# Row maxima of two attention heads, taken together from two neighbouring PSUM banks

## The reference

```python
q = _heads(xq @ wq)
k, v = jnp.split(ctx @ wkv, 2, axis=-1)
...
sim = jnp.einsum('bhnd,bhmd->bhnm', q, k) * DH ** (-0.5)
a = jax.nn.softmax(sim, axis=-1)
o = jnp.einsum('bhnm,bhmd->bhnd', a, v)
```

## Time and profile before

| | us |
|---|---|
| median of three runs | 6196.47 |
| lowest, highest | 6185.82, 6211.56 |
| profiled execution | 6242.82 |
| its span | 6241.0 |

### The profile page before, as it was taken

The page is one execution under the profiler, slowest core; times in us unless marked ns, Lnnn a source line. Parts: engine busy times, 40 slices in busy tenths (PEclk is TensorE's granted clock), DMA queues, the critical chain, the costliest instruction groups (busy, mean ns, idle before and its releaser), DMA issues. The chain is left out here.

```text
span 6241.0 us, 170025 instructions
## 1 busy us (share of the span) xinstructions
PE 5692.5 (91%) x66584; PEld 3349.0 (54%) x66584; DVE 4360.4 (70%) x8986; ACT 3383.1 (54%) x7674; POOL 2505.9 (40%) x2223
## 2 busy tenths in 40 slices
PE   6999899988899989998889998999888998899988
PEld 4566346643556635664356653566435665356633
DVE  6886666656788666665788867666668886666664
ACT  3455565546544556554644556555564555655555
POOL 2566016730256501673026640277103663037700
PEclk9999699987899969998899987999779998699976
DMA  4000010000100001000010000100001000010000
GB/s 111 23 16 17 13 30 16 13 20 12 44 23 16 15 15 32 14 14 18 16 44 22 16 18 12 32 13 15 19 17 45 13 16 17 11 36 13 7 17 8
DMA packets 277771, 135.56 MB, mean 22 GB/s; under 512 B 151005, under 2 KB 266301, under 8 KB 276862
## 3 DMA queue, kind: packets, MB, share of 16 engines
q1 hardware_dynamic: 276990, 124.68, 8.5%
HBM read 101.90 MB, written 3.01 MB: 17 GB/s over the span
## 5 line engine op out<-in xcount | busy, mean ns | idle before, releaser
L2266 DVE TENSOR_REDUCE max_part<-ring 128x1 f32<-128x400 f32 (+2 forms) x4608 | 2418.6, 578 | 776.1 <-PE ring L1425 768.0
L1918 ACT ACTIVATE probs<-ring 128x512 f32<-128x512 f32 (+1 forms) x4096 | 2101.2, 572 | 1337.9 <-PE ring L1425 1312.4
L1401 POOL TENSOR_TENSOR weight_sum<-weight_sum,probs 128x512 f32<-128x512 f32 (+1 forms) x1408 | 1793.7, 1274 | 150.3 <-ACT probs L1918 11.5
L1425 PE MATMUL o_acc<-probs,region 128*32 128x256 f32 (+2 forms) x13312 | 1503.1, 441 | 47.2 <-ACT probs L1918 41.4
L1425 PEld LDWEIGHTS o_acc<-probs,region 128*32 128x32 f32 (+2 forms) x13312 | 617.2, 133 | 573.8 <-issue 262.4
L1401 POOL TENSOR_TENSOR weight_sum<-probs 128x512 f32<-128x512 f32 x256 | 332.1, 1297 | 1467.7 <-PE ring L1425 923.6
L1425 PE MATMUL ring<-qop,region 64*128 64x256 f16 x9984 | 833.1, 270 | 22.6 <-ACT shift_q L1763 16.7
L1763 ACT ACTIVATE region<-ring 65x128 f32<-65x128 f32 (+4 forms) x1232 | 560.9, 474 | 413.8 <-PE ring L1425 319.8
L1425 PE MATMUL ring<-nk,nq 32*128 32x400 f16 (+2 forms) x2560 | 601.9, 401 | 65.2 <-ACT probs L1918 51.1
L1425 PEld LDWEIGHTS ring<-qop,region 64*128 64x128 f16 x9984 | 522.2, 95 | 188.2 <-issue 92.1
L1425 PE MATMUL ring<-shift_q,shift_k 64*128 64x256 f16 (+1 forms) x3840 | 618.3, 270 | 0.0
(11 more groups left out here) (181 smaller groups left out, 6668.6 us busy)
## 6 DMA issues: line engine op xcount, KB each, us to landing
stage<-in_wide SPq DMA_DIRECT2D x448, 64.0 KB, 1.9
nk<-region SPq DMA_DIRECT2D x768, 25.0 KB
wo_stage<-in_wide SPq DMA_DIRECT2D x32, 512.0 KB, 4.0
stage<-in_wide SPq DMA_DIRECT2D x64, 128.0 KB, 2.5
v_stage<-in_wide SPq DMA_DIRECT2D x128, 64.0 KB, 1.9
ff_w<-in_ff_w SPq DMA_DIRECT2D x24, 256.0 KB, 3.3
stage<-kv_split SPq DMA_DIRECT2D x64, 96.0 KB, 2.1
v_stage<-kv_split SPq DMA_DIRECT2D x128, 48.0 KB, 1.7
```

What stands on the lines that cost most here:

```text
L1401: pool.tensor_tensor(total, before, probs[0:rows_, (un.chunk + k) % PROBS, :], ALU.add)\
L1425: return pe.matmul(out, lhs, rhs, start=start, stop=stop, skip_group_check=True)
L1918: act.activation(to, src, ACT.Exp, scale=t.scale).then_inc(exp_done.sem, 1)
L2266: dve.tensor_reduce(dst, src, AX.X, ALU.max).then_inc(*release(one))
```

## The change

A max job is now one for two neighbouring heads: PE writes the first head's scores into one bank and the second's into the next bank, alternating between the heads, and VectorE reduces both banks with one instruction. The list of jobs, the estimates of the planner and the weights of due times follow. In Plan.run a max job needs two banks that lie side by side, of which the first has an even number (side_by_side, pick); scores take such a pair when there is one; single jobs prefer a bank whose neighbour is taken. RING goes from 4 to 5. A bank's former users can now be two, so room() gives a list of waits; every wait is for the former user itself, and the first free marks on VectorE go. A "scale" (the division on GpSimd) is kept from being due earlier than the one before.

```diff
-POOL_BANKS, RING, SLOTS, PROBS = 7, 4, 4, 8
+POOL_BANKS, RING, SLOTS, PROBS = 7, 5, 4, 8
...
-            return [("max", (h, q), k) for q in range(QT) for h in range(2)]
+            return [("max", (0, q), k) for q in range(QT)]
...
-        out = [("max", (h, q), k) for q in range(QT) for k in range(len(self.kc)) for h in range(4)]
+        out = [("max", (h, q), k) for q in range(QT) for k in range(len(self.kc)) for h in (0, 2)]
...
-                costs.append({"spread": 0.4, "op": width * 0.0018, "low": 0.0, "val": 1.2, "max": 0.5}[kind])
+                costs.append({"spread": 0.4, "op": width * 0.0018, "low": 0.0, "val": 1.2, "max": 1.0}[kind])
...
-                put(at + (1.5 if last else 3.0), "scale", n)
+                done["scale"] = max(at + (1.5 if last else 3.0), done.get("scale", at) + 0.0001)
+                put(done["scale"], "scale", n)
...
-            self.part("PE", "max", due, one, 0.1 if t.cross else 0.16, deps, 0.25)
+            self.part("PE", "max", due, one, 0.2 if t.cross else 0.32, deps, 0.25)
...
-            self.part("DVE", "max", due, one, 0.58 if t.cross else 0.68, [pe, *old])
+            self.part("DVE", "max", due, one, 1.0 if t.cross else 1.24, [pe, *old])
...
         def takes(what):
-            if what[0] == "scores":
+            if what[0] == "scores" or is_max(what):
                 return 2
             return int(what[0] in ("pre", "job"))
+
+        def partner(r):
+            return r ^ 1
+
+        def side_by_side():
+            return [r for r in banks if r % 2 == 0 and r + 1 in banks]
+
+        def pick(what):
+
+            pairs = side_by_side()
+            if takes(what) == 2 and pairs:
+                found = [pairs[0], pairs[0] + 1]
+            else:
+                found = sorted(banks, key=lambda r: partner(r) in banks)[:takes(what)]
+            for r in found:
+                banks.remove(r)
+            return found
...
-                        if len(banks) < takes(what) or held[use] + takes(what) > {"ring": RING, "scores": SLOTS}[use]:
+                        if len(banks) < takes(what) or is_max(what) and not side_by_side():
+                            continue
+                        if held[use] + takes(what) > {"ring": RING, "scores": SLOTS}[use]:
                             continue
...
-            before = PLAN.before[one]
-            if before and before[0] == "scores":
-                return emptied(before[1])
-            r = slot_free[bank(one)]
-            return r.sem, r.at("all", RING_AT[one][2])
+            return [emptied(before[1]) if before[0] == "scores" else taken(before) for before in PLAN.before[one]]
...
+                    if kind == "max":
+                        h0, q = i
+                        a0, w = t.kc[k]
+                        for m, qq in enumerate(range(QT) if q is None else [q]):
+                            for h in range(2):
+                                part = slice(64 * h, 64 * h + 64)
+                                last = mm(ring[:, bank(one) + h, m * w:(m + 1) * w], qop[part, z, 0, qq * P:(qq + 1) * P],
+                                          kop_of(un)[part, 0, a0:a0 + w], True, True)
...
-            for r in range(POOL_BANKS):
-                dve.sem_inc(slot_free[r].sem, 1)
...
+                        both = ring[:, bank(one):bank(one) + 2, :]
                         if q is None:
-                            src = ring[:, bank(one), 0:QT * w].rearrange("p (q k) -> p q k", q=QT)
-                            dst = max_part[:, n % 2, 2 * h:2 * h + 2, 0]
+                            src = both[:, :, 0:QT * w].rearrange("p h (q k) -> p h q k", q=QT)
+                            dst = max_part[:, n % 2, 2 * h:2 * h + 4, 0].rearrange("p (h q) -> p h q", q=QT)
                         else:
-                            src, dst = ring[:, bank(one), 0:w], max_part[:, n % 2, 2 * h + q, k:k + 1]
+                            src, dst = both[:, :, 0:w], max_part[:, n % 2, 2 * h + q:2 * h + q + 3:2, k]
                         dve.tensor_reduce(dst, src, AX.X, ALU.max).then_inc(*release(one))
```

More of the change, by code:

```diff
@@ L699, in run, with is_max @@
         events, now, left, tiled = [], 0.0, len(self.parts), (P, P)
+        def is_max(what):
+            return what[0] == "job" and UNITS[what[1]].t.jobs[what[2]][0] == "max"
         def takes(what):
-            if what[0] == "scores":
+            if what[0] == "scores" or is_max(what):
                 return 2
             return int(what[0] in ("pre", "job"))
+        def partner(r):
[11 more added lines that the diff above has]
+            return found
         while left:
@@ L761, in run @@
                     left -= 1
-                    if (e, what) in owner:
-                        r, use = owner.pop((e, what))
+                    for key in [key for key in owner if key[0] == (e, what)]:
+                        r, use = owner.pop(key)
                         banks.append(r)
@@ L1054, in room_for_scores @@
             if before and before[0] == "scores":
-                return emptied(before[1])
-            return taken(before) if before else (slot_free[r].sem, slot_free[r].at("all"))
+                return [emptied(before[1])]
+            return [taken(before)] if before else []
         def score_bank(g):
@@ L1498, in pre @@
                         stored(s, u, m - 1)
-                    free, value = room(one)
-                    pe.wait_ge(free, value)
+                    for free, value in room(one):
+                        pe.wait_ge(free, value)
                     out = ring[:, bank(one), :]
@@ L1677, in narrow_job @@
                     else:
-                        h, q = i
+                        h0, q = i
                         a0, w = t.kc[k]
                         for m, qq in enumerate(range(QT) if q is None else [q]):
-                            part = slice(32 * h, 32 * h + 32)
-                            last = mm(out[:, m * w:(m + 1) * w], nq[part, z, qq * P:(qq + 1) * P], nk[part, z, a0:a0 + w],
-                                      True, True)
+                            for h in (h0, h0 + 1):
+                                part = slice(32 * h, 32 * h + 32)
+                                last = mm(ring[:, bank(one) + h - h0, m * w:(m + 1) * w], nq[part, z, qq * P:(qq + 1) * P],
+                                          nk[part, z, a0:a0 + w], True, True)
                     last.then_inc(job_full.sem, 1)
@@ L1694, in make_scores @@
                     for one in (g, g + 1):
-                        pe.wait_ge(*room_for_scores(one))
+                        for free, value in room_for_scores(one):
+                            pe.wait_ge(free, value)
                     side, nz = P // t.heads, un.narrow_at % NK_SLOTS
```

37 lines of the change are left out of this document (15 added, 22 removed).

## The result

The changed kernel takes 6306.44 us (median of four runs, 6304.05 to 6315.16), the kernel before 6192.93 (four runs, 6185.82 to 6211.56): ratio 1.0182, 95% interval 1.0161 to 1.0203. The forecast was 6157 with a range of 6095 to 6260. The profiled execution took 6305.17 us, its span is 6303.4 and the mean clock 0.885 (before 6242.82, 6241.0, 0.898).

A forecast was written before the change was run, and what follows sets the result against it. The prediction took PE's work to bound wide cross, a chain narrow cross, and VectorE to be longest in wide self. Terms -8 - 38 - 5 + 12 = -39 from the median 6196.5 gave 6157 us, range 6095 to 6260.

The forecast's parts named there:

- VectorE's part: Maxima on VectorE: two-bank instructions of 966 and 1,190 ns, 2,304 fewer instructions, 230 to 382 us less busy time.
- Wide self, -8: Wide self attention: two maxima become one of 1.19 us, 8 us less in all (0 to -15).
- First wide cross, -38: First wide cross stage: paired maxima cost PE 0.6 us less in each of 64 units, 38 us less.
- rival 4: PE's 0.34 us idle ahead of a unit's first scores goes too; with other favourable ends -106 us, 6090; chance 0.10.
- The prediction's worst end, 0: First wide cross: no gain if pairs stand alone as single maxima do now, six blocks alone costing 0.6 us.
- Second wide cross, -5: Second wide cross stage: maxima already better packed, at most 0.17 us a unit to gain, 5 us less (0 to -11).
- Narrow self, 0: Narrow self attention: four maxima a unit and gaps everywhere, so no change (-6 to +6).
- Narrow cross, +12: Narrow cross: a late pair delays the values 0.4 us in some 30 of 448 cycles, +12 us (-20 to +180).
- Rival 1: Narrow cross: a late pair stands before the values in half the cycles, 100 us more, 6245 in all; chance 0.20.
- rival 3: Clock of the narrow stages shifts ten points, 45 us either way, 6202 or 6112; chance 0.07 colder, 0.06 warmer.
- Rival 2: Pairs wait for neighbouring banks and stand alone; wide cross gains only a few us, 6180; chance 0.20.
- Rival 5: The two-bank maximum costs twice a single one; VectorE saves nothing, wide cross keeps its gain, 6165; chance 0.02.

The follow-up runs named there:

- pairs_wide: The changed kernel with pairs of heads in the wide attentions alone, single maxima in the narrow ones, RING 5: 6143.03 us, ratio 0.9911 to the kernel before.
- pairs_cross: The changed kernel with pairs in wide cross attention alone, everything else single, RING 5: 6147.86 us, ratio 0.9923 to the kernel before.
- before_ring5: The kernel before with RING at 5 and nothing else changed: 6156.11 us, ratio 0.9926.
- cross_ring4: The changed kernel with pairs in wide cross attention alone and RING at 4: 6188.13 us, ratio 0.9988 to the kernel before.
- singles_ring6: The changed kernel without any pairs and with RING at 6: 6463.46 us, ratio 1.0431 to the kernel before.
- half_columns: The changed kernel, same order, but in narrow cross VectorE reads only the first 200 of each bank's 400 columns: 6189.10 us, ratio 0.9982 to the kernel before.
- any_neighbours: The changed kernel, but a pair may begin at any bank whose next one is free, odd ones too: 6370.39 us, ratio 1.0275 to the kernel before.

## Why the prediction was wrong, point by point

**VectorE's part: near in each duration, too high in the sum.** 987 and 1,210 ns against 966 and 1,190. Its busy time fell by 131 us, where 230 to 382 were foretold. In a row singles come closer than the 0.50 us that I used: 25 in 12.13 us in before, (12.13 - 0.57) / 24 = 0.482 apart, against nine pairs in 8.18 us in after, (8.18 - 0.99) / 8 = 0.899; a pair spares 0.065 us, and 2,304 x 0.065 = 150. The maxima's own busy time fell by 149 us.

```profile
2212.97 12.13 DVE L2266 TENSOR_REDUCE max_part<-ring 128x1 f32<-128x400 f32 x25 [0.84 <-PE ring L1425]
```

```profile
2204.53 8.18 DVE L2287 TENSOR_REDUCE max_part<-ring 128x2 f32<-128x800 f32 x9 [0.61 <-PE ring L1444]
```

**Wide self, -8: not seen.** pairs_wide differs from pairs_cross by the pairs of wide self, and its wide stages together are 3824 us against 3812: +12 in place of -8. Each is one trace, and the narrow cross stages of the kernels with single maxima there and RING at 4 or 5 differ by as much (1696 to 1708), so this says that no gain was seen, not that there is a loss.

**First wide cross, -38: the direction was right, the size too small, and the fifth bank left out.** A pair beside scores costs 0.18 (1807.22 to 1807.40) and alone 0.27 (1804.39 to 1804.66), as read from the earlier trace rows:

```profile
1804.39 0.34 PE L1444 MATMUL ring<-region,qop 64*128 64x400 f16 x2
1804.66 0.86 PE L1444 MATMUL ring<-v_stage,src_t 96*64 96x128 f16 x24
...
1807.22 0.34 PE L1444 MATMUL ring<-region,qop 64*128 64x400 f16 x2
1807.40 0.49 PE L1444 MATMUL ring<-qop,region 64*65 64x256 f16 x6
```

The maxima of a unit fell by 0.75 us (0.6 foretold; the prediction read 2.17 us of maxima in one unit, the count above has 2.45), and other work by as much again. Of that, 0.34 us is idle time of PE, a piece of rival 4, which is gone in before_ring5 too; a unit also has 26 changes of tile shape for 27, and the rest wasn't placed. The prediction's worst end, 0, doesn't follow from its own prices: 1.36 + 6 x 0.10 = 1.96 is still 0.2 under 2.17, so 13 us. But of the 60 us that the two first stages gained, before_ring5 has 61 without a pair. On top of it the pairs of pairs_cross gain 10 us in twelve units of each round, and give back 3 where the batch element changes (34.9 us where it was 32.8) and in the last unit: 28 us in four rounds. Another 16 go at the start of the two stages, and 12 are left. The term that was mis-sized is RING: I gave the fifth bank nothing, as a mere condition of the pairs. By the two first stages it alone gives 61 us, the pairs alone 29 (cross_ring4), both 73 (pairs_cross); by the program 0.7%, 0.1% with an interval that holds 1, and 0.8%.

**Second wide cross, -5: the direction was right,** the size not (-14; the range went to -11). **Narrow self, 0: -14, outside its range.**

**Narrow cross, +12: the step that failed.** The prediction priced one form, a late pair ahead of the values in some 15 cycles (30 x 0.4), and said that a pair costs nothing if it is issued ahead of the second scores. I counted what PE waits for VectorE (over 0.1 us) ahead of narrow maxima outside the long blocks, in all 448 cycles: ten times and 1.5 us in before, 97 times and 47 us in after. Of the 97 only 30 stand ahead of the values, 18 us: the count foretold, at 0.6 us each. 67 stand ahead of scores, 29 us: the place that the prediction called free. It isn't, for the second scores stand behind such a pair, and behind them the exponentials. In the first narrow cross stage of round 2 these waits are 0.2 to 0.9 us long. Waits ahead of the values whose bank comes from ScalarE, as in the cycle shown above, became fewer (109 and 35 us in before, 18 and 17 us in after), but PE's waits for the exponentials themselves, ahead of scores and values, grew from 105 to 161 us. And a second form was missing: pairs that find no two banks in cycle after cycle and land in a block at a unit's end, which with the blocks at the start makes +62 us.

I argued from the due times that the pairs would find their place. But by the code of Plan.run a pair whose due time comes isn't taken when one bank is free, and single jobs with a later due time can take the bank. Plan.run can be run alone in Python, with its estimates and without the chip. It then passes over a ready narrow cross pair 2,039 times with one bank free and 599 times with two that are not such a pair (the single maxima of before are passed over only for the limit of four or with no bank free). Cut into the same stages, its narrow cross takes 1617 us for before and 1718 for after, **101 of the 152 us measured**, and 1817 for singles_ring6 (200 of 249). With 0.58 us on VectorE for a cross pair in place of 1.0 the plan still has 1711: there it is the two banks at once that cost, more than the time that they are held. On the chip that isn't shown. Two thirds of the loss could so be read before the launch. The plan's end hides it, 6251 and 6257 us, as the wide stages gain what narrow cross loses.

Rival 1 has the right stage and the right direction. Its condition, a pair before the values in half the cycles, wasn't met: pairs stand right before the values in 127 of 448 cycles (single maxima did in 228). That the cycles lost 91 us, near its 100, is luck. The blocks were in no rival. With -77 of the wide stages, -14 of narrow self and +152 the span of 6241.0 goes to 6302, as measured.

**The clock.** The granted clock of the narrow cross stages over four rounds went from 0.74 and 0.75 to 0.71 and 0.69. By the prediction's reading the time at the low clock is (0.52 x 846 + 0.50 x 859) = 870 us before and (0.58 x 918 + 0.62 x 939) = 1,115 after. With a cycle of 3.65 us at the one and 2.65 at the other, 245 us more at the low clock are 67 us: an estimate from above, as the longer stages themselves are part of these 245 us. How much of the 152 us is the clock and how much the waits isn't separated by any run; in half_columns the clock was 0.73 in both. The direction of rival 3 (colder) is right; the clock fell together with the longer waits.

**Rival 2** had pairs stand alone in wide cross for want of banks that lie side by side. In wide cross that didn't cost the gain (a unit is 1.49 us shorter); in narrow cross pairs do wait for banks, but not for the even first one (any_neighbours). **Rival 5** fell: a two-bank read of 400 columns in all takes 571 ns (half_columns), one of 400 in one bank 566.

What stays open: how the 152 us divide between the order and the hold (75 us stay with the short hold), the 50 us between the profiled execution of before and its median, and the share of the clock.

The best kernels are those without narrow pairs: pairs_wide 0.9911, pairs_cross 0.9923, before_ring5 0.9926. Their intervals lie over each other, so on the evidence the simplest, one number changed in the kernel before, is as good as any. Plan.run alone orders them so too: 6157 us for before_ring5, 6143 for pairs_wide, 6145 for pairs_cross.

## What to carry to other kernels

A merged instruction that saves an engine time can cost the pool of buffers more: it takes two at once and gives both back late. Count the free banks of the tightest cycle (here seven less four at scores less two at a pair), ask what stands behind the job that finds too few, and look also for jobs that find none and pile up at the end. Where the order is planned ahead, read the plan's own time stage by stage before the launch: here it held two thirds of the loss, and its end alone showed nothing. When a change widens a limit to make room for itself, run the wider limit alone first; and widen it by one more to see where it turns (4 to 5 gained 0.7%, 6 lost 4.3%; the kernel with 6 differs from before in more than RING, but Plan.run gives before with RING at 6 an end of 6359 us and that kernel 6368).

## What was not expected of the hardware

One VectorE instruction over two PSUM banks has no extra price: 987 ns for 2 x 400 columns and 571 ns for 2 x 200, against 566 for 400 in one bank, so some 1.04 ns a column and about 155 ns for the instruction. Two matmuls of two heads in different row groups start together, and the pair costs PE the same 0.17 to 0.18 us beside scores as one did. VectorE's singles in a row stand 0.48 us apart at 566 ns each, pairs 0.90 at 987: the overlap between neighbours is 84 to 88 ns, the same for either.
